# Routed token rows exchanged between partitions by DMA and turned in 32x32 squares by VectorE, in place of TensorE transposes

## The reference

```
x = x + tanh(g_xattn) * mamba(ctx, z = layernorm(x))     # selective scan, 512 channels, 16 states, 512 steps, 4 batches
x = x + tanh(g_ffn)   * moe(layernorm(x))
moe(h): scores = softmax(h @ gate_w.T); the best 6 of 16 experts, weights divided by their sum
        y = sum over chosen e of c_e * (silu(h @ W1_e.T) * (h @ W3_e.T)) @ W2_e.T      # inner width 352
        y = y + the same with a shared expert of inner width 704
```

## Time and profile before

| | |
|---|---|
| median of 3 runs (lowest, highest) | 1439.08 us (1438.27, 1440.55) |
| profiled execution, span | 1435.5 us |
| PE busy, mean granted clock | 1349.9 us (94%), 0.976 |
| DVE, ACT, POOL busy | 787.5, 730.9, 949.3 us |
| DMA, mean | 104 GB/s |

### The profile page before, as it was taken

One profiled execution on the slowest core, in us unless ns is written; L12 is line 12 of the kernel. 1 busy time (PEld: TensorE's weight loads), 2 busy tenths in 40 slices (PEclk: granted clock), 3 DMA queues, 4 the chain that ended last, 5 costly groups with the idle time before them and its releaser, 6 DMA issues.

```text
span 1435.5 us, 32257 instructions
## 1 busy us (share of the span) xinstructions
PE 1349.9 (94%) x8480; PEld 1210.6 (84%) x8481; DVE 787.5 (55%) x1364; ACT 730.9 (51%) x1317; POOL 949.3 (66%) x671
## 2 busy tenths in 40 slices
PE   6897998997898899999999999999999999999996
PEld 2686887887888799999998989989889988899885
DVE  6878898898989854653333333333333333333331
ACT  5898897898889464343332333323333333332321
POOL 0588898898988747887456665566645666546632
PEclk8899999999999999999999999999999999999999
DMA  4120122222242365645455435555445544454432
GB/s 137 38 74 31 53 67 96 67 73 91 75 146 72 133 129 106 142 84 141 83 141 145 131 63 144 139 147 137 104 94 137 141 135 104 95 147 131 76 68 36
DMA packets 65042, 149.13 MB, mean 104 GB/s; under 512 B 16976, under 2 KB 17616, under 8 KB 62656
## 3 DMA queue, kind: packets, MB, share of 16 engines
q0 software_dynamic: 31024, 62.10, 22.9%
q1 hardware_dynamic: 33392, 81.21, 17.5%
q10 hardware_dynamic: 560, 4.98, 1.0%
HBM read 101.50 MB, written 48.99 MB: 105 GB/s over the span
## 4 chain that ended last, share of the span: by engine, by line
PE 65%; DVE 3%; issue 1%; POOL 0%; ACT 0%; DVEq 0%; POOLq 0%; ACTq 0%
PE bank L1719 19%; PE bank L1699 19%; PE bank L1700 18%; PE bank L1687 3%; PE bank L1710 3%; DVE hs L1172 1%; PE bank L1604 1%; PE bank L1590 1%; PE bank L1602 0%; POOL hc L949 0%; DVE sc L1226 0%; PE bank L1665 0%; DVEq L1375 0%; DVE xl L1363 0%; DVE du L1186 0%
## 5 line engine op out<-in xcount | busy, mean ns | idle before, releaser
L949 POOL TENSOR_TENSOR hc<-hs,crow 128x512 f32<-128x512 f32 x254 | 322.6, 1302 | 91.8 <-DVE hs L1172 84.6
L1699 PE MATMUL bank<-w,xh 128*128 (+1 forms) x1088 | 368.7, 340 | 7.6 <-issue 4.2
L1015 POOL DMA_INDIRECT out_x<-ys,aid x104 | 171.2, 1646 | 275.0 <-issue 215.7
L1700 PE MATMUL bank<-w,xh 128*128 (+1 forms) x1088 | 351.2, 323 | 0.0
L1172 DVE TENSOR_TENSOR_SCAN hs<-dA,bank 128x512 f32<-128x512 f32 x256 | 295.8, 1208 | 47.9 <-PE bank L1604 32.0
L1719 PE MATMUL bank<-w,ah 128*128 (+1 forms) x816 | 264.7, 405 | 2.7 <-DVE al L1399 2.7
L1399 DVE TENSOR_TENSOR al<-bank,ah 128x384 fp32r<-128x384 f32 x136 | 75.8, 557 | 331.0 <-ACT ah L862 283.2
L1699 PEld LDWEIGHTS bank<-w,xh 128*128 128x128 f32 x1088 | 204.3, 188 | 35.9 <-issue 32.1
L1700 PEld LDWEIGHTS bank<-w,xh 128*128 128x128 f32 x1088 | 206.4, 190 | 2.3
L868 ACT COPY ys<-bank 128x512 f32<-128x512 f32 x136 | 79.9, 587 | 195.9 <-PE bank L1719 191.5
L1700 PE MATMUL bank<-w,xl 128*128 (+1 forms) x544 | 175.9, 323 | 0.0
(11 more groups left out here) (184 smaller groups left out, 2051.7 us busy)
## 6 DMA issues: line engine op xcount, KB each, us to landing
wraw<-in_wall SPq DMA_DIRECT2D x16, 2176.0 KB
crow<-c_rows SPq DMA_DIRECT2D x64, 256.0 KB, 3.3
xt<-token_rows_turned SPq DMA_DIRECT2D x32, 256.0 KB
out_x<-ys POOLq DMA_DIRECT2D x32, 256.0 KB
wraw<-in_wall ACTq DMA_DIRECT2D x2, 2176.0 KB
token_rows<-rowb SPq DMA_DIRECT2D x4, 1028.0 KB
xrow<-in_x SPq DMA_DIRECT2D x4, 1024.0 KB, 7.0
out_x<-xrow SPq DMA_DIRECT2D x4, 1024.0 KB, 4.9
```

The costliest lines, as they stand in the source:

```text
L949: nc.gpsimd.tensor_tensor(hc[:, j, :], hs[:, j, :], crow[:, n % 4, :], ALU.mult).then_inc(hc_done, 1)
L1015: pool.indirect_dma_start(out_rows, bass.IndirectOffsetOnAxis(ap=aid[:, s:s + 1], axis=0), ys[:, s, :], None, bounds_check=TOKENS - 1, oob ...
L1699: nc.tensor.matmul(gate_bank[:, 0:I], xx, columns(w, off + ww + k * 2 * I, I), start=first, stop=last)
L1700: mm = nc.tensor.matmul(up_bank[:, 0:I], xx, columns(w, off + ww + k * 2 * I + I, I), start=first, stop=last)
```

## The change

`turn_x` is gone from TensorE. A gathered tile now lies in `rowg`, a token on each partition. For each pair of tiles, once both are gathered, SyncE issues 16 transfers from SBUF to SBUF (`exchange`), one for each pair of partition quadrant q and column quadrant c: 32 partitions, two tiles, 128 columns, 32 KB each, into `xq`. VectorE then turns all of a tile's 32x32 squares by one instruction (`turn`) from `xq` into PSUM bank 4, where TensorE's transposes went before. `xh`, `xl` and all after them are as before. For this the features of a stored row stand in another order, so `rows` writes them by 16 transfers with pieces of 32 floats (and one for the last two columns) where one transfer of whole rows did.

Moved with it: every `fetch` of raw weights goes to GpSimd's queue (experts 4 to 17 by an instruction behind `split_low`, found through a new row 5 of `meta`); gathers are issued 7 tiles early; `gather` waits for its slot's exchange (`swapped`) and not for `xt_turned`; token numbers are taken from tile 26 on (VectorE now waits for `ids_in` ahead of tile 26) and the first gathers stand at GpSimd's tiles 27 to 31; the 24 `list_tokens` are packed so that the last stands at tile 21, and the table is read at tile 22. `take_weight` is for t+2.

```diff
-AHEAD = 5
-FIRST_ROWS = {NS - 3: (NS, NS + 1), NS - 2: (NS + 2,), NS - 1: (NS + 3, NS + 4)}
+QUAD = P // 32
+AHEAD = 7
+FIRST_IDS = {NS - 6: (NS, NS + 1), NS - 5: (NS + 2, NS + 3), NS - 2: (NS + 4,), NS - 1: (NS + 5,)}
+FIRST_ROWS = {NS - 5: (NS, NS + 1), NS - 4: (NS + 2, NS + 3), NS - 3: (NS + 4,), NS - 2: (NS + 5,), NS - 1: (NS + 6,)}
+LISTED_AT = {**{t: (t - 2,) for t in range(2, 15)}, 15: (13, 14), 16: (15,), 17: (16, 17), 18: (18,), 19: (19, 20), 20: (21,), 21: (22, 23)}
+LISTS_READ = 22
+FETCHES = {TT - 3: 2, NS - 3: 3}
...
+        rowg = alloc(ctx, "rowg", [P, 4, ROW])
+        xq = alloc(ctx, "xq", [P, 4, H])
...
             def rows(b, _):
                 sp.wait_ge(norm_done, TC * (b + 1))
-                sp.dma_start(rows_v[b, :, :, 0:H + 2], rowb[:]).then_inc(rows_stored, 16)
+                with nc.allow_non_contiguous_dma(reason="a row's columns by quadrant of the transposed row"):
+                    for t in range(TC):
+                        for c in range(QUAD):
+                            sp.dma_start(rows_v[b, :, t, c * P:(c + 1) * P].rearrange("p (k i) -> p k i", k=HK),
+                                         rowb[:, t, 0:H].rearrange("p (k c i) -> p c k i", k=HK, c=QUAD)[:, c]).then_inc(rows_stored, 16)
+                    sp.dma_start(rows_v[b, :, :, H:H + 2], rowb[:, :, H:H + 2]).then_inc(rows_stored, 16)
...
-            with sp.Fori(3, NX) as e:
-                fetch(e)
+            def exchange(i, h):
+
+                for s in (2 * h, 2 * h + 1):
+                    apart(sp, gathered[s], 16 * i + 16, "sp")
+                apart(sp, xt_turned, 4 * i + NS + 2 * h - 2, "sp")
+                for q in range(QUAD):
+                    for c in range(QUAD):
+                        sp.dma_start(xq[32 * c:32 * c + 32, 2 * h:2 * h + 2, q * P:(q + 1) * P],
+                                     rowg[32 * q:32 * q + 32, 2 * h:2 * h + 2, c * P:(c + 1) * P]).then_inc(swapped[h], 16)
+
             sp.wait_ge(meta_ready, 2)
+            groups = routed_groups(sp)
+            with sp.Fori(0, groups) as i:
+                for h in range(2):
+                    exchange(i, h)
...
+            def fetch(e):
+
+                at_least(pool, wl_done, e)
+                pool.dma_start(wraw[:], wall[e]).then_inc(raw_in, 16)
...
-            def gather(t, s):
-
-                if isinstance(t, int) and t < NS + 4:
-                    pool.wait_ge(xl_done, t - 3)
-                else:
-                    apart(pool, xt_turned, t - 3, "pool")
+            def gather(t, s, before=0):
+
+                if not (isinstance(t, int) and t < NS + 4):
+                    apart(pool, swapped[s // 2], 16 * QUAD * QUAD * before, "pool")
                     apart(pool, cc_done, t - 3, "pool")
                 apart(pool, gid_done, t + 1, "pool")
-                pool.indirect_dma_start(xt[:, s, :], None, rows_d[:, :],
+                pool.indirect_dma_start(rowg[:, s, :], None, rows_d[:, :],
                                         bass.IndirectOffsetOnAxis(ap=gid[:, s:s + 1], axis=0)).then_inc(gathered[s], 16)
...
                 e = pool.value_load(meta[0:1, 2, bass.ds(t, 1)], min_val=0, max_val=NX - 1)
                 with pool.If(e > 0):
                     split_low(e)
+                f = pool.value_load(meta[0:1, 5, bass.ds(t, 1)], min_val=0, max_val=NX - 1)
+                with pool.If(f > 0):
+                    apart(pool, wl_done, f, "pool")
+                    pool.dma_start(wraw[:], wall[bass.ds(f, 1)].rearrange("a p c -> p (a c)")).then_inc(raw_in, 16)
...
+            def turn(t, s4, before):
+
+                if isinstance(t, int) and t < NS:
+                    return
+                apart(dve, swapped[s4 // 2], 16 * QUAD * QUAD * (before + 1), "dve")
+                dve.wait_ge(xh_done, t)
+                dve.wait_ge(xl_done, t)
+                nc.vector.transpose(banks[4][:].rearrange("p (k q j) -> p q k j", k=HK, q=QUAD),
+                                    xq[:, s4, :].rearrange("p (q k i) -> p q k i", q=QUAD, k=HK)).then_inc(xt_turned, 1)
...
-            def tile(t, s4, gathers=False, adds=False, m=None):
+            def tile(t, s4, group=0, gathers=False, takes=False, adds=False):
                 s = s4 % 2
+                turn(t + 1, (s4 + 1) % 4, (t + 1 - NS) // 4 if isinstance(t, int) else group + s4 // 3)
                 a_low(t - 1, 1 - s)
-                take_weight(t + 1, (s4 + 1) % 4, m)
...
-                if t == NS - 3:
+                if t == min(FIRST_IDS):
                     dve.wait_ge(ids_in, 16)
...
-            def turn_x(t, s, m=None):
-                rows_in(pe, t, s, m, "pe")
-                at_least(pe, xl_done, t)
-                for k in range(HK):
-                    mm = nc.tensor.transpose(banks[4][:, k * P:(k + 1) * P], xt[:, s, k * P:(k + 1) * P], ident[:])
-                mm.then_inc(xt_turned, 1)
```

112 lines of the change are left out of this document (60 added, 52 removed).

## The result

| | before | changed |
|---|---|---|
| median of the runs, us | 1438.67 (1437.77 to 1440.55, 4 runs) | 1497.1 (1494.99 to 1501.21, 4 runs) |
| span of the profiled execution, us | 1435.5 | 1493.3 |

A forecast was written before the change was run, and what follows sets the result against it. TensorE was taken to bound the kernel, with slack in every other engine. On the 1435.5 us span, -45.8 + 14.7 + 1.7 + 1.0 = -28.4 gave 1407.1; with 3.6 us over the span, 1411 us was forecast, range 1390 to 1434.

The forecast's parts named there:

- the sum: Whole kernel: -45.8 + 14.7 + 1.7 + 1.0 = -28.4 us on the span of 1435.5, so 1407.1 us.
- the pause: Ahead of tile 26: VectorE waits for the token-number table, TensorE stands still 14.7 us once, plus 1.7 for the clock.
- 45.8 us go: Third stage: 104 routed tiles each lose 0.44 us of TensorE's work when `turn_x` goes.
- 19 us ahead of need: SyncE's exchange: may begin some three tiles or 19 us before its tiles are wanted, so its 10.2 us fit.
- The turn, the transposes, the start: VectorE's turn takes 0.7 us in idle time; TensorE's transposes of gathered tiles vanish; `rows`' extra issues cost zero.
- DMA contention: Third stage: the DMA engines' share rises from 0.49 to between 0.62 and 0.78, contention but no bound.
- The 0.44 us: TensorE's saving per routed tile, the period 6.74 us with `turn_x` against 6.30 us without.
- nothing but TensorE: Chain of waits in both stages of expert tiles: only TensorE, `down`s 6.30 us apart for shared tiles, 6.74 for routed.
- 0.45 us a transfer: SyncE's issue time for each of an exchange's 16 transfers, or 7.2 us a pair.
- 0.84 us: SyncE's queue time per transfer above which the changed kernel gets slower than the kernel before.
- SyncE cannot keep up: Rival for the third stage: slow transfers on SyncE's queue make the kernel slower, 1569 us in its example; chance 0.10.
- The rival of the fetches: Fetches in GpSimd's queue delay adds and gathers, 1.5 us at each of 14 experts: +21 us, 1432 us; chance 0.22.

The follow-up runs named there:

- e16: e12 with TensorE's register reads for the next tile moved between `up` and `turn_a`, except at every fourth tile: 1454.97 us, ratio 1.0102.
- e12: Changed kernel with 12 of 16 transfers per exchange, half of `split_low` from expert 3 on, and `x_low` directly behind `a_low`: 1442.43 us, ratio 1.0033.
- e3: Changed kernel with four of the 16 transfers of each exchange left out: 1466.03 us, ratio 1.0196.
- e5: Changed kernel with `split_low` computing only half of the low parts from expert 3 on: 1452.94 us, ratio 1.0118.
- e6: Changed kernel with `split_low` cut into four pieces, one in each of an expert's first four tiles, nothing left out: 1462.21 us, ratio 1.018.
- e1: Changed kernel with all weight fetches off GpSimd's queue, fetch 0 on SyncE and the rest on ACT: 1494.96 us, ratio 1.0391.
- e4: Kernel before with only its fetches moved to GpSimd's queue; TensorE still transposes: 1433.56 us, ratio 0.9967.
- e18: e4 with TensorE's register reads for the next tile moved between `up` and `turn_a`: 1474.4 us, ratio 1.0255.

## Why the prediction was wrong

Against the sum, on the span: 1407.1 us forecast, 1493.3 measured, 86 us more. The long intervals make 62 of them (65.0 less 0.16 x 15; some 16 of these are the lower clock), the ordinary tiles 89 x (6.77 - 6.46) = 28, the pause with its clock 1; the start of the kernel takes back 1.5 us and its end 3. The mechanism failed, not only a size: two steps, "45.8 us go" and "19 us ahead of need", took engines and buffers to have slack that they had not.

- **The turn, the transposes, the start.** Right. L1417 takes 0.73 us (0.7 forecast) in idle time, the transposes are gone, the first stage lost nothing, and the median was 3.8 us over the span.
- **The pause.** Right in place, cause and size: to tile 31 the changed kernel loses 17.3 us, for 14.7 + 1.7. The granted clock was 0.50 from 666.7 to 683.8 us, and `down(25)` took 3.76 us for 2.09. What the sum lacks is the same price behind the waits of the third stage, 16 us as estimated above; with the granted clock at 0.97 between 720 and 1400 us it is easily passed over.
- **DMA contention.** Right: the mean share rose from 0.49 to 0.62 (800 to 1400 us), the lower of the two values given, and e16's tiles of 6.3 us run beside the exchange.
- **"45.8 us go."** Wrong, and it is the term that the forecast rested on. The 0.44 us are TensorE's, and e16 shows its floor at 6.26 to 6.29 us. But the period was bounded by several things at nearly the same height. In the kernel before, `down` starts 1.0 us after the end of `a_low` (rows below), as TensorE has `turn_x` to do; in the changed one 0.6 us (969.92 + 0.56 = 970.48, and 971.07). TensorE's queue waits for `a_low` ahead of `down` (its next entry starts at 910.47 us and at 970.52, just behind that end), and the reads stand behind `down`; so `turn_x` gave it time over which to begin the reads, and without it they begin later against `down` (0.45 us for 0.15) and end behind it. That they are what fills the gap is shown by e16 and by the step from `down` to `up`, and the share of the loop over `x_low` (some 9 us) by e12. The rows of the kernel before, timelines of DVE and PE:

```profile
909.88 0.56 DVE L1399 TENSOR_TENSOR al<-bank,ah 128x384 fp32r<-128x384 f32 x1 [2.46 <-issue]
...
911.46 0.71 PE L1719 MATMUL bank<-w,ah 128*128 x2
```

  The sign stood in the trace of the kernel before, and the prediction read it as "nothing but TensorE". Between 745 and 1400 us 3.3% of the chain are other things, 12 us of "issue" and VectorE's reads and `x_low` among them, and TensorE's weight loads already waited ahead of `up` 67 times. Two pieces of the chain (DVEq L1375 is a read of `gather_ids`), and the waits of 745 to 1420 us:

```profile
932.42 0.80 DVEq L1375
933.82 0.70 DVE xl L1363
```

```profile
PEld bank L1699 <- issue: 29.7, 67, 1.2
```

- **"An exchange may begin some 19 us ahead of need."** Wrong, and the largest part. I worked from the wait on `turn` alone. The exchange also waits for its gathers, the gather for the exchange two pairs earlier (`swapped`), and both stand in queues that hold other work. The ring holds two pairs, so one round may take 2 x 12.6 = 25.2 us. Gathers one tile apart (6.3 us), 4 us to land, 10.3 us of exchange and 2 to 3.5 us to its landing (landings by the chain of waits, 1370 to 1450 us) make 22.6 to 24.1 us of that, and leave nothing for `split_low`'s 9.6 us. e3, e5 and e6 show both parts.
- **0.45 us a transfer.** Mis-sized: 0.60, and 0.64 from start to start. It is under the 0.84 us at which I let SyncE decide, because that point was worked out without the waits; the rival "SyncE cannot keep up" named the right queue and the wrong condition. The rule of the Trainium skill cited there ("SBUF — State Buffer", The DMA setup-cost knee), about 2 us for each transfer, would have made 33 us a pair if they stood in series, an estimate from that page. The 16 transfers were issued in 10.3 us and had landed 2 to 3.5 us later, so that cost was not paid in series.
- **The rival of the fetches.** Its waits came (59.3 us for adds), yet by e1 taking the fetches away gains 2 us, within the spread of the runs, and by e4 the fetches alone cost nothing.

## What to carry to other kernels

Taking work from the engine that bounds is worth only the distance to the next bound: add up the loops through the other engines and the engine's own register reads before the whole period is booked as gain, and compare with a period measured in a stage that has the same reads. For a ring of buffers write down the recurrence round the ring, with every queue that it crosses, before speaking of reserve; what matters is not how early a transfer may start by one semaphore. Give every expected stall of TensorE the price of the lower clock behind it. And if removing a wait leaves the time as it was, look at the intervals that are *not* long.

## What the runs showed of the hardware

- A transfer of 32 KB, 32 partitions from SBUF to SBUF, takes 597 ns of SyncE's queue in the median (588 the least), 0.64 us from start to start, longer than the 0.37 to 0.43 us of most issues in the earlier trace rows.
- VectorE's transpose of 32x32 squares, 128x512 f32 from SBUF to PSUM, takes 0.73 us.
- A register read in TensorE's queue takes 0.3 us, and from the first of two to the next weight load 1.8 us pass. Put ahead of `turn_a` they made the kernel before slower by 41 us (e18 against e4): its weight loads waited there 69 times for 46.8 us, where in e4 they waited 56 times for 24.3 us ahead of `up`.
- Behind a stall of 4.3 us TensorE's granted clock was 0.50 for 3.4 us, and its matmuls of `up` followed each other by 0.29 us, where it is 0.16 at 1.00.
- A fetch of 2176 KB on GpSimd's queue is issued in 0.58 us and lands 9.0 us later; an add behind it landed 9.3 us after its own issue, and that cost nothing here.
